# First gathered tile transposed ahead of the last output projection and the last normalisations, last block's logits one expert tile later

## Time and profile before

| | us |
|---|---|
| median of 3 runs | 621.26 (620.62 to 621.82) |
| profiled execution | 622.48 |
| its span, first to last instruction | 620.8 |

### The profile page before, as it was taken

The page is one execution under the profiler, slowest core; times in us unless marked ns, Lnnn a source line. Parts: engine busy times, 40 slices in busy tenths (PEclk is TensorE's granted clock), DMA queues, the critical chain, the costliest instruction groups (busy, mean ns, idle before and its releaser), DMA issues. The chain is left out here.

```text
span 620.8 us, 9016 instructions
## 1 busy us (share of the span) xinstructions
PE 566.4 (91%) x2452; PEld 421.6 (68%) x2453; DVE 542.3 (87%) x862; ACT 428.8 (69%) x806; POOL 271.6 (44%) x217
## 2 busy tenths in 40 slices
PE   0786788999999999999999999999998999999991
PEld 0565565667668767776866876786466878788880
DVE  6978898999999899899999989899999699777770
ACT  4636475577767759767766865966886777788872
POOL 2165454461454445355245454512032364756631
PEclk9888889999999999999999999999996999999996
DMA  8273063028108404701910840477654576877740
GB/s 299 111 184 86 1 167 37 1 83 216 42 1 231 110 0 175 146 18 40 246 51 0 226 112 2 149 188 273 180 190 151 174 235 210 260 229 226 233 157 0
DMA packets 40980, 84.41 MB, mean 136 GB/s; under 512 B 8751, under 2 KB 8751, under 8 KB 40818
## 3 DMA queue, kind: packets, MB, share of 16 engines
q1 hardware_dynamic: 30482, 56.67, 27.4%
q0 software_dynamic: 10464, 27.33, 19.7%
HBM read 66.95 MB, written 35.65 MB: 165 GB/s over the span
## 5 line engine op out<-in xcount | busy, mean ns | idle before, releaser
L1110 POOL TENSOR_TENSOR mixed<-unsplit,mixed 128x1024 fp32r<-128x1024 f32 x44 | 106.4, 2439 | 149.4 <-ACT mixed L762 149.4
L516 PE MATMUL kb<-mixed,w_kvr 128*128 128x512 f32 x384 | 98.4, 407 | 20.7 <-DVE w_kvr L1450 14.1
L516 PE MATMUL vb<-mixed,w_kvr 128*128 128x512 f32 x384 | 101.6, 415 | 10.9 <-DVE evn L1292 10.8
L692 PE MATMUL y_ps<-w_e_hi,xgT 128*128 x312 | 109.0, 411 | 0.1
L516 PE MATMUL rb<-mixed,w_kvr 128*128 128x512 f32 x384 | 100.3, 411 | 4.7 <-DVE ee L1306 4.7
L529 PE MATMUL y_ps<-w_o,rw 128*128 128x512 f32 x224 | 100.8, 594 | 0.0
L516 PEld LDWEIGHTS kb<-mixed,w_kvr 128*128 128x128 f32 x384 | 73.7, 195 | 39.5 <-issue 13.8
L516 PEld LDWEIGHTS vb<-mixed,w_kvr 128*128 128x128 f32 x384 | 73.4, 196 | 32.3 <-DVE evn L1292 14.3
L516 PEld LDWEIGHTS rb<-mixed,w_kvr 128*128 128x128 f32 x384 | 73.0, 192 | 26.2 <-DVE ee L1306 5.9
L1126 POOL TENSOR_TENSOR ee<-ee,state 128x512 f32<-128x512 f32 x32 | 34.9, 1091 | 91.7 <-DVE state L1276 90.9
L1243 DVE SCALAR_TENSOR_TENSOR unsplit<-diff,vec,xb 128x512 f32<-128x512 f32 x96 | 65.8, 747 | 6.4 <-PE kb L516 6.1
(11 more groups left out here) (230 smaller groups left out, 1020.2 us busy)
## 6 DMA issues: line engine op xcount, KB each, us to landing
bias<-b_experts SPq DMA_DIRECT2D x39, 256.0 KB, 4.5
x_biased<-bo POOLq DMA_DIRECT2D x8, 1024.0 KB, 17.3
w_e_raw<-w_experts SPq DMA_DIRECT2D x8, 1024.0 KB, 7.9
rows<-x_biased SPq DMA_DIRECT2D x28, 256.0 KB, 3.6
x_rows<-rows SPq DMA_DIRECT2D x28, 256.0 KB, 6.6
xb<-xT SPq DMA_DIRECT2D x4, 1026.0 KB, 5.3
xb<-xT SPq DMA_DIRECT2D x3, 1024.0 KB, 5.2
w_raw<-w_square SPq DMA_DIRECT2D x2, 1024.0 KB, 10.8
```

The lines of the kernel that those rows point to most:

```text
L516: mm = pe.matmul(bank, w_kvr[m][:, a, h, o:o + P], mixed[m][:, bb, h, :], start=(k == 0), stop=(k == 3 * CH - 1))
L692: mm = pe.matmul(y_ps[:, n % 2, :], xgT[n % 3][:, a, c, :], w[:, bass.ds(p, 1), c, :].rearrange("p u o -> p (u o)"), start=(c == 0 and (a, ...
L1110: pool.tensor_tensor(mixed[m][:, LO, 2 * hp:2 * hp + 2, :], unsplit[m][:, LO, 2 * hp:2 * hp + 2, :], mixed[m][:, HI, 2 * hp:2 * hp + 2, :] ...
```

## The change

On TensorE the last quarter of the last block's output projection moves behind the first gathered tile's transposes, and the last block's transposes and logits move one expert tile later:

```diff
             turn_rows(before, 2)
-            out_last(3)
             logits(before, 2, late_ps[:, 2, :])
             turn_rows(before, 3)
             pe.wait_ge(d_ready, CHUNKS)
             turn(0, 0, 0)
+            out_last(3)
             logits(before, 3, late_ps[:, 3, :])
             turn(1, 0, 1)
...
-                if k == 0:
+                if k == 1:
                     turn_last(0)
                     turn_last(1)
-                if k == 1:
+                if k == 2:
                     logits_last(0)
                     logits_last(1)
                     turn_last(2)
                     turn_last(3)
-                if k == 2:
+                if k == 3:
                     logits_last(2)
                     logits_last(3)
```

On ScalarE `move_gathered` is defined earlier, and the order becomes:

```diff
             expert_hi(6)
+            move_turned(before, 2)
+            move_turned(before, 3)
+            move_gathered(0, 0)
             deviation_last(0)
             norm_last(0)
-            move_turned(before, 2)
-            deviation_last(1)
-            norm_last(1)
-            move_turned(before, 3)
...
-            move_gathered(0, 0)
             move_gathered(1, 1)
             act.wait_ge(y_filled, TILES)
             expert_hi(7)
+            deviation_last(1)
+            norm_last(1)
+            move_gathered(2, 2)
             deviation_last(2)
             norm_last(2)
             deviation_last(3)
             norm_last(3)
-            move_gathered(2, 2)
-            move_last(0)
-            move_last(1)
             for k in range(FULL):
                 move_gathered(k + 3, (k + 3) % RING)
                 if k == 0:
+                    move_last(0)
+                    move_last(1)
+                if k == 1:
                     move_last(2)
                     move_last(3)
```

On VectorE four of the weight splits move behind the first gathered tiles:

```diff
             expert_lo(2)
-            expert_lo(3)
-            expert_lo(4)
-            expert_lo(5)
...
             split_gathered(0, 0)
             add_last(2)
+            expert_lo(3)
+            split_gathered(1, 1)
             add_last(3)
-            split_gathered(1, 1)
+            expert_lo(4)
+            expert_lo(5)
             expert_lo(6)
             expert_lo(7)
             add_bias(0, 0, 0)
```

More of the change, by code:

```diff
@@ L1002, in move_last, with move_gathered @@
                 act.activation(x1T_last[:, j % 2], last_banks[j % 2].rearrange("p (c q) -> p c q", c=CH), ACT.Copy).then_inc(x1T_moved, 1)
+            def move_gathered(k, n):
+                act.wait_ge(turned, k + 1)
+                wait(act, expert_filled, k - 2)
+                act.activation(xgT[n % 3][:, HI], turned_ps[n % 2], ACT.Copy).then_inc(turned_hi, 1)
             reciprocal_guess(before, 1)
```

## The result

| | before | changed |
|---|---|---|
| median of 20 runs, us | 621.24 | 623.76 |
| lowest and highest | 620.02 to 622.81 | 621.11 to 627.46 |
| profiled execution | 622.48 | 625.90 |
| its span | 620.8 | 624.2 |

The ratio is 1.0045, with a 95% interval of 1.003 to 1.0061: the change costs 2.5 us (predicted: 2.1 against the median). The runs also scatter over 6.4 us where they scattered over 2.8.

A forecast was written before the change was run, and what follows sets the result against it. TensorE bounds the expert phase, entered through VectorE's gapless queue. Order -0.3 plus low clock 1.8 gives +1.5; with the 0.6 correction, 2.1 on the 621.26 median: 623.3 us, range 621.2 to 625.3.

The forecast's parts named there:

- TensorE's head start: At expert(0): TensorE starts four us sooner, then loses it idling 5.7 us before turn(4); as a rival, surviving, -6.4, chance 0.05.
- VectorE's new wait of 1.0 us before split_gathered(1): VectorE stands still from 467.0 to 468.0 us, waiting for TensorE's turn(1) and ScalarE's copy; ends 0 and 2.7.
- the second rival: Clock falls twice: out_last(3) also slow, 1.7 us more before split_gathered(1), reaching turn(4), +3.2 in all; chance 0.25.
- The low clock at expert(2): After the idle stretch before turn(4), expert(2) runs at the low clock, costing 1.8 us, ends 1.5 and 2.6.
- split_gathered(0) without a wait, at 463.4: VectorE's first split follows expert_lo(2) directly, 6.6 us sooner than its old 470.03, since TensorE and ScalarE are early enough.
- The likeliest case, one fall: The main forecast: the clock is low only at expert(2), after TensorE's idle stretch; 623.3 us, chance 0.55.
- two falls: Clock low at out_last(3) and again at expert(2): +1.5 + 1.7 = +3.2 us, 625.1 us against the median; chance 0.25.
- the fixed point: Reference in the handover: end of expert(2) with logits_last(0), (1) and turn_last(2), (3), at 486.78 us before the change.
- The correction of 0.6: Profiled kernel before lost 2.4 us to the clock at expert(0), usually 1.8; so 0.6 added to the cost against the median.
- the first rival: Held clock: the level survives the idle stretch before turn(4), giving -0.3 or -1.3, 620.0 to 621.0 us; chance 0.15.
- what delays TensorE at the door is not won back: Expert phase, 484 to 600 us: TensorE is busy 114.94 of 116 us, so any delay on entering it stays.
- ScalarE's part and SyncE's queue: Costs nothing: norm2(1) waits for the last transposes, delaying add_gathered(2) harmlessly; bias of tile 1 arrives with 1.4 us to spare.

The follow-up runs named there:

- a1: Changed kernel with VectorE's old order (four expert_lo ahead of split_gathered(0)), TensorE and ScalarE keeping the new order: 621.03 us, ratio 1.0005 to the kernel before.
- c2: Changed kernel with the last block's transposes and logits back at their old tiles, ScalarE's moves accordingly, VectorE's new order kept: ratio 0.9990 to the kernel before.
- a3: Changed kernel with 22 extra matmuls on TensorE behind turn_last(1), in the idle stretch before turn(4): 621.82 us, ratio 1.0017 to the kernel before.
- b1: Changed kernel with extra matmuls: 12 in the early list, 2 and 1 in waits before turn(0), 22 before turn(4): 624.33 us, ratio 1.0056 to before.
- b2: Changed kernel with only the early extra matmuls (list and waits before turn(0)), without the 22 before turn(4): 626.73 us, ratio 1.0095 to before.
- x1: Changed kernel with logits at their old tiles and three expert_lo ahead of split_gathered(0): 618.64 us, ratio 0.9970 to the kernel before.
- x3: x1 with the biases of tiles 1 and 2 loaded ahead of the last block's stores in SyncE's queue: 625.76 us, ratio 0.9946 to the kernel before.
- b3: Kernel before with 3 extra matmuls behind turn(0), 12 behind turn(1), and the tile-list wait moved ahead of turn(0): 619.79 us, ratio 0.9982 to before.
- c1: Kernel before with only 12 extra matmuls in TensorE's early list: 628.99 us, ratio 0.9993 to the kernel before on the same chip.

## Why the prediction was right

- *TensorE's head start is given back before turn(4).* Right: idle 5.71 us in both profiles, released by VectorE's split each time. The prediction says 5.7; its own times, 474.6 and 480.15, give 5.55. a1 and c2 show that both halves are needed for the loss: VectorE's splits ahead of split_gathered(2), and the logits behind the gap.
- *VectorE's new wait of 1.0 us before split_gathered(1).* Right in size: 0.98 in the first profile, 0.92 in a3 and 1.02 in c2, which have the same order up to there. In the second profile of the changed kernel it is 2.73, the second rival's.
- *The low clock at expert(2).* Right: 4.56 us instead of 2.86, 1.7 against 1.8 predicted. The fill that keeps the clock up is worth 1.7 us by a3 and 2.4 by b1 and b2.
- *split_gathered(0) without a wait, at 463.4.* Right in the second profile, in a3 and in c2; in the first it waited 2.60 us. My reason, TensorE early enough, held only for a clock that had not fallen in the list. I had looked for a fall between 458.7 and 462.4 and not ahead of the change.
- *The likeliest case, one fall.* Both profiles of the changed kernel show two falls, the case that I gave 0.25, and in the first the early one lies where I had not looked. Seven profiles (these two, a1, a3, c2, x1, x3) share TensorE's order up to out_last(3) without early fills, and two of the seven have an early fall. Of the changed kernel itself no profile shows the one-fall case. Its first profiled execution is 2.1 us above the median, its second 0.6 below that of its chip, so they don't tell which case a median execution is. For two falls the sum of 3.2 fits the second profile (3.3 at the fixed point). In the first, where the early fall cost 2.60 us of waiting and not 1.7, it is 4.3 there and 3.4 in the span. Over the first 20 runs the time goes with the mean granted clock: at 0.970 and above 621.11 to 623.75 us, below it 623.69 to 627.46 (correlation -0.82).
- *The number, 2.1 predicted and 2.5 measured.* The median mixes the cases, so the closeness is in part luck. The correction of 0.6 took 1.8 us as the usual price of the clock in the kernel before; b3 measured 1.1, which would make the correction 1.3 and the forecast 2.8. The same 0.6 was left out of the first rival's 620.0 to 621.0.
- *That what delays TensorE at the door is not won back.* Not quite: 4.3 us later at the fixed point became 3.4 in the span, mostly because TensorE no longer waited for gathers behind it (0.28 instead of 1.06 us idle from 490 to 600).
- *The wider scatter* was not predicted. b1, b2, b3 and c1 show its basis: the new order passes on what TensorE loses before turn(0), the old one swallowed it. That the early falls are the source in single runs fits the narrow scatter of b1 and b2, and is not shown.
- *ScalarE's part and SyncE's queue.* As said, norm2(1) waited for the last transposes (VectorE stood 4.99 us ahead of add_gathered(2)), and TensorE had no wait for it. The bias of tile 1 caused no wait in either profile of the changed kernel. The 1.4 us to spare were not tested there.

## What to carry to other kernels

Before an early consumer is moved ahead, follow the producer's queue to the third item, not the first: here expert(0) and expert(1) came 1.3 and 4.5 us sooner, but the split of tile 2, behind four weight splits, came 3.8 us later, so the engine that sets the time only got a gap. Work that is ready belongs into such a gap and not behind it, and long independent passes of another engine are the cover for a late one; spread them so that each hand-over keeps one. Here a gap of 5.7 us on TensorE cost twice, once as idle time and once as slow matmuls behind it. And read more than one profile: the first and the second of this kernel had their early fall of the clock at different places.

## What the runs showed of the hardware

- In the changed kernel's first profile the granted clock fell in the early list although TensorE was busy 3.40 of 3.40 us by the records: 24 matmuls of 32 columns and logits of 8, with weight loads of 3.04 us. In the kernel before and in eight further profiles it stayed at 1.00 through the same code. TensorE's work up to the fall is the same in all ten, so neither the order nor the busy time in the records tells which execution has one.
- Useless matmuls can pay: 22 of them in a 5.7 us gap made the changed kernel 1.7 us faster (2.4 by b1 against b2), 15 made the kernel before 1.1 us faster. 12 in a stretch without a gap cost TensorE their full 2.8 us, and whether the kernel pays them depends on the cover: b1 is 2.4 us above a3, c1 no slower than before.
